# A Flamingo block: the last attention batch in an order of its own, its last pair's sums on VectorE

## The reference

```python
x = x + tanh(g_xattn[0]) * xattn(ctx, layernorm(x), Wq, Wkv, Wout, gm, bm, gl, bl)
x = x + tanh(g_ffn[0]) * ffn(layernorm(x), W_fc, W_proj)

def xattn(x, latents, ...):             # here x is ctx, latents is layernorm(x)
    xn = layernorm(x, gm, bm); ln = layernorm(latents, gl, bl)
    q = ln @ Wq;  k, v = split(concat([xn, ln]) @ Wkv)     # 8 heads of 64
    sim = (q / scale) @ k.T;  attn = softmax(sim - max(sim))
    return (attn @ v) @ Wout
def ffn(x, W_fc, W_proj):
    y = square(relu(x @ W_fc.T)) @ W_proj.T
    # five steps: mem = 0.9*mem + y - reset*1.0, spike = mem > 1.0; the mean of the spikes is returned
```

## Time and profile before

| | us |
|---|---|
| median of 3 runs | 1161.47 (1161.38 to 1162.35) |
| the profiled execution, its own time | 1163.12 |
| its span, first to last instruction | 1161.3 |
| of it: up to the end of the output projection of b = 6, the loop's last | 722.8 |
| the last batch (b = 7), to the start of `up(0, 2)` | 102 |
| the feed-forward part from there | 336.5 |

### The profile page before, as it was taken

The page is one execution under the profiler, slowest core; times in us unless marked ns, Lnnn a source line. Parts: engine busy times, 40 slices in busy tenths (PEclk is TensorE's granted clock), DMA queues, the critical chain, the costliest instruction groups (busy, mean ns, idle before and its releaser), DMA issues.

```text
span 1161.3 us, 19261 instructions
## 1 busy us (share of the span) xinstructions
PE 1082.1 (93%) x7117; PEld 886.2 (76%) x7117; DVE 763.2 (66%) x1138; ACT 535.6 (46%) x999; POOL 376.5 (32%) x336
## 2 busy tenths in 40 slices
PE   2999999999999999999999999865899999999992
PEld 2987887877877877877887887643688788788991
DVE  4247877877777776787687686655433556456498
ACT  4346745844845754754764764332333322322321
POOL 1003433443353353353344434343112122122232
PEclk9789999999999999999999999977899999999996
DMA  5300201200101101101100000121430100200201
GB/s 171 106 23 1 70 1 32 69 0 32 69 0 32 60 9 32 49 19 32 36 33 29 3 0 23 46 82 57 132 109 1 37 1 19 73 1 6 87 2 54
DMA packets 31334, 47.42 MB, mean 41 GB/s; under 512 B 2240, under 2 KB 10448, under 8 KB 31296
## 3 DMA queue, kind: packets, MB, share of 16 engines
q1 hardware_dynamic: 31296, 46.91, 12.5%
HBM read 39.56 MB, written 7.34 MB: 40 GB/s over the span
## 4 chain that ended last, share of the span: by engine, by line
PE 87%; DVE 7%; DMA 2%; POOL 1%; ACT 1%; issue 1%; SPq 0%; DVEq 0%; ACTq 0%; POOLq 0%
PE work L421 50%; PE score L729 11%; PE heads_out L540 8%; PE score L504 8%; PE score L436 2%; PE maxes L661 2%; PE heads_out L549 1%; PE maxes L526 1%; PE maxes L516 1%; DMA xin<-in_ctx 1%; DVE neuron L1385 1%; DVE neuron L1383 1%; POOL dsum L1452 1%; DVE spikes L1381 1%; PE score L421 1%
## 5 line engine op out<-in xcount | busy, mean ns | idle before, releaser
L1452 POOL TENSOR_TENSOR dsum<-dsum,probs 125x448 f32<-125x448 f32 (+1 forms) x192 | 235.9, 1229 | 15.1
L1449 POOL TENSOR_TENSOR dsum<-probs 125x448 f32<-125x448 f32 x32 | 37.0, 1157 | 468.8 <-ACT probs L807 468.8
L421 PE MATMUL work<-wv,xT 128*125 128x512 f32 (+1 forms) x768 | 188.7, 400 | 0.0
L421 PE MATMUL work<-xT,wk 128*128 128x488 f32 (+1 forms) x768 | 188.2, 396 | 0.0
L421 PE MATMUL work<-zT,wf 128*128 128x512 f32 (+1 forms) x768 | 168.5, 371 | 13.2 <-DVE wf L1208 12.2
L421 PEld LDWEIGHTS work<-wv,xT 128*125 128x125 f32 (+1 forms) x768 | 139.0, 184 | 37.4 <-issue 2.3
L421 PEld LDWEIGHTS work<-xT,wk 128*128 128x128 f32 x768 | 142.7, 191 | 31.1 <-issue 4.6
L729 PE MATMUL score<-hT,wp 128*128 128x512 f32 (+1 forms) x768 | 163.8, 363 | 0.6 <-DVE hT L1404 0.6
L421 PEld LDWEIGHTS work<-zT,wf 128*128 128x128 f32 x768 | 134.9, 193 | 37.4 <-issue 14.1
L801 ACT ACTIVATE probs<-score 125x448 f32<-125x448 f32 (+1 forms) x256 | 119.9, 549 | 75.3 <-PE score L504 75.1
L1494 POOL TENSOR_TENSOR h<-relu 128x512 f32<-128x512 f32 (+1 forms) x64 | 71.5, 1118 | 247.0 <-ACT relu L1030 242.6
(11 more groups left out here) (135 smaller groups left out, 1312.8 us busy)
## 6 DMA issues: line engine op xcount, KB each, us to landing
xin<-in_ctx SPq DMA_DIRECT2D x48, 250.0 KB
neuron<-in_L_ffn_W_fc SPq DMA_DIRECT2D x16, 256.0 KB, 4.5
neuron<-in_L_ffn_W_proj SPq DMA_DIRECT2D x16, 256.0 KB, 2.7
xin<-in_x SPq DMA_DIRECT2D x16, 224.0 KB, 9.8
xres<-in_x SPq DMA_DIRECT2D x16, 224.0 KB, 2.6
x_scratch<-xres SPq DMA_DIRECT2D x16, 224.0 KB, 2.3
zt<-x_scratch SPq DMA_DIRECT2D x3, 1024.0 KB, 5.7
fin<-x_scratch SPq DMA_DIRECT2D x3, 1024.0 KB, 5.6
```

What stands on the lines that cost most here:

```text
L421: mm = pe.matmul(bank, lhs(i, k), rhs(j, k), start=(n == 0), stop=(n == len(passes) * chunks - 1))
L1449: pool.tensor_tensor(total[0:CT], tile(0), tile(1), ALU.add).then_inc(dchain, 1)
L1452: pool.tensor_tensor(total[0:ROWS[t]], total[0:ROWS[t]], tile(t), ALU.add).then_inc(dchain if t < TILES - 1 else dsum_done, 1)
```

## The change

Four things are changed, all in or next to the last batch.

1. SP issues `load_z(0, False)` directly behind the loop, ahead of `residual(NA - 2)`, and without the wait for `tr_done`.
2. PE, ACT and DVE have lists of their own for the last batch. DVE makes only the statistics of group 0; ACT makes the negated means, the variance plus epsilon and the four normalisations, and POOL one product more (`nmr`). On PE, `max_transposes(1)` and `max_rows(1)` come ahead of values 4 and 5; `max_transposes(2)`, `max_rows(2)` ahead of the third scores; `max_transposes(3)` and `max_rows(3)` ahead of `up(0, 1)` and of `attend(2)`. On ACT, `heads_hi(1)` moves from ahead of the last pair's first copies to behind the last exponentials, and the copy of value tile 3 to behind `exponentials(1)`. On DVE, `normalise(1)` moves to behind `subtract(7)`.
3. The last pair's exponentials are summed by DVE (`last_sums`, four instructions) instead of POOL's seven.
4. The last pair's value products and totals go to the bank `maxes`, so `attend(3)` no longer waits for `on_done`.

```diff
@@ sync
-            residual(NA - 2, False)
+            load_z(0, False)
+            residual(NA - 2, False)
...
-            sp.wait_ge(tr_done, NA * 2 * DC)
-            load_z(0, False)
@@ tensor, last_batch
-                now_until_queries(b)
+                max_transposes(b, 1)
+                values(b, 4)
+                max_rows(b, 1)
+                values(b, 5)
...
+                max_transposes(b, 2)
                 attend(b, 1)
+                max_rows(b, 2)
                 totals(b, 1)
-                max_transposes(b, 2)
                 scores(b, 3, 0, last=True)
-                max_rows(b, 2)
                 scores(b, 3, 1)
                 up(0, 0, False)
+                max_transposes(b, 3)
+                max_rows(b, 3)
+                up(0, 1, False)
                 attend(b, 2)
                 totals(b, 2)
-                max_transposes(b, 3)
-                up(0, 1, False)
-                max_rows(b, 3)
-                attend(b, 3)
-                totals(b, 3)
+                attend(b, 3, maxes)
+                totals(b, 3, maxes)
@@ scalar, last_batch
+                exponentials(b, 1)
+                copy_values(b, 3, 4, 5)
...
+                heads_hi(b, 0)
+                group_hi(0, 0, 1, 2, 3)
+                split_weights(0)
+                copy_scores(b, 3, 0, 1)
+                exponentials(b, 4)
+                split_weights(1)
+                copy_scores(b, 3, 2, 3)
+                exponentials(b, 5)
+                exponentials(b, 6)
+                exponentials(b, 7)
+                heads_hi(b, 1)
+                split_weights(2, 3)
+                heads_hi(b, 2)
...
@@ vector
+            def last_sums(b):
+                v = probs[:, 2:4, :]
+                dve.wait_ge(exp_done, b * HEADS + HEADS)
+                dve.tensor_tensor(top[0:CT], v[0:CT, :, 0:2 * L], v[0:CT, :, 2 * L:4 * L], ALU.add)...
+                dve.tensor_tensor(top[0:CT], top[0:CT], v[0:CT, :, 4 * L:6 * L], ALU.add)...
+                dve.tensor_tensor(top[0:LT], top[0:LT], v[0:LT, :, 6 * L:8 * L], ALU.add)...
+                dve.tensor_tensor(dsum[0:CT, 2:4, :], top[0:CT, :, 0:L], top[0:CT, :, L:2 * L], ALU.add)...
@@ vector, last_batch
+                group_lo(0, 0, 1, 2, 3)
+                subtract(b, 4)
+                split_weights(0)
+                folds(b, 3, 1)
+                subtract(b, 5)
+                folds(b, 3, 2, 3)
+                maxima(b, 3)
+                split_weights(1)
+                query_maxima(b, 3)
+                subtract(b, 6)
+                subtract(b, 7)
+                normalise(b, 1)
+                heads_lo(b, 1)
+                last_sums(b)
+                split_weights(2)
+                normalise(b, 2)
+                heads_lo(b, 2)
+                split_weights(3)
+                normalise(b, 3, maxes)
+                heads_lo(b, 3)
+                split_weights(4, 5, 6, 7)
```

More of the change, by code:

```diff
@@ L633, in last_batch @@
             def last_batch(b):
-                now_until_queries(b)
+                max_transposes(b, 1)
+                values(b, 4)
+                max_rows(b, 1)
+                values(b, 5)
+                keys_queries(b, 2, (2,))
+                values(b, 6)
+                values(b, 7)
+                attend(b, 0)
+                totals(b, 0)
+                scores(b, 2, 0)
+                keys_queries(b, 3, (0,))
+                scores(b, 2, 1)
+                keys_queries(b, 3, (1, 2))
                 for i in range(4):
@@ L909, in batch @@
                 copy_scores(b, 2, 2, 3)
[L910 to L911 removed]
+                layer_norm(b + 1, 1)
                 kq_hi_parts(b, 3, 1)
[L913 to L927 removed]
                 hi_chunks(b + 1, 0, 0)
@@ L1209, in split_weights, with last_batch, batch @@
                                       ALU.subtract).then_inc(fw_lo, 1)
-            def batch(b, last):
-                if not last:
-                    statistics(b + 1, 0)
-                    statistics(b + 1, 1)
-                else:
-                    group_statistics(0, False)
+            def last_batch(b):
+                query_maxima(b, 1)
+                group_moments(0, False)
+                subtract(b, 2)
+                kq_lo_parts(b, 2, 2)
+                subtract(b, 3)
+                latent_values(b, 6)
+                latent_values(b, 7)
+                normalise(b, 0)
+                folds(b, 2, 1)
+                kq_lo_parts(b, 3, 0)
+                folds(b, 2, 2, 3)
+                maxima(b, 2)
+                kq_lo_parts(b, 3, 1, 2)
+                heads_lo(b, 0)
+                query_maxima(b, 2)
+                group_lo(0, 0, 1, 2, 3)
[19 more added lines that the diff above has]
+                split_weights(4, 5, 6, 7)
+                for i in range(2):
+                    gated_residual(b, i)
+            def batch(b):
+                statistics(b + 1, 0)
+                statistics(b + 1, 1)
                 query_maxima(b, 1)
@@ L1347, in _ @@
             with dve.Fori(0, NA - 1) as b:
[L1348 to L1349 removed]
+                batch(b)
+            last_batch(NA - 1)
             def neuron_op(g, n, last):
@@ L1470, in batch @@
                 else:
-                    inverse_root(g_ve, 1, g_rstd, 0, 4)
-                for p in range(1, PAIRS):
+                    inverse_root(g_ve, 1, g_root, 0, 4)
+                    pool.wait_ge(g_root, 1)
+                    pool.tensor_tensor(nmr[:, 0:4], nmu[:, 0:4], rstd[:, 0:4], ALU.mult).then_inc(g_rstd, 1)
+                for p in range(1, PAIRS - 1 if last else PAIRS):
                     denominators(b, p)
```

117 lines of the change are left out of this document (52 added, 65 removed).

## The result

| us | before | after |
|---|---|---|
| median of 4 runs | 1161.91 (1161.38 to 1165.62) | 1134.9 (1134.71 to 1135.9) |
| profiled execution | 1163.12 | 1135.09 |
| its span | 1161.3 | 1133.3 |

The ratio is 0.9763, with a 95% interval of 0.9741 to 0.9784. The forecast was 1132.7, with a range of 1128 to 1140.

A forecast was written before the change was run, and what follows sets the result against it. TensorE's waits in the last batch's 102 us, a third idle and paid twice through a lower clock, were the bound. +0.75 - 5.05 + 0.5 - 23.3 - 1.7 = -28.8 from 1161.47 gave 1132.7, range 1128 to 1140.

The forecast's parts named there:

- To `attend(0)`: Start of the last batch: value tile 3 later, +0.75; no wait for zt or qmax and faster values 7, -5.05.
- To the last scores: From attend(0) to the last pair's scores: TensorE already full, only max_rows(2) comes in, +0.5 us.
- To the last exponential: From the last scores to the end of the last exponential: 17.7 us in place of 41.0, -23.3, VectorE's chain setting it.
- three moves: Basis of the -23.3: normalise(1) behind the subtractions, heads_hi(1) behind the exponentials, maxima ahead of attend(2).
- To the projection: From the last exponential to the output projection: 13.0 us in place of 14.7, -1.7, the tree's saving mostly lost to queueing.
- The projection: Last batch's output projection: 3.1 us of idle time ahead of it remain, so it keeps 7.20 us, no change.
- A: Rival on TensorE's granted clock: full clock gives 1130.6, inside the main forecast's 0.72; low clock gives 1139, chance 0.09.
- the middle case: Main sum's clock level: attend(2) at half-clock price, 5.17 us, attend(3) at 3.25 and the projection at 7.20, giving 1132.7.
- B: Rival: GpSimd's pair 2 sums run on under VectorE's tree, tree and splits cost +4.5 to +6, 1138; chance 0.09.
- The rule: VectorE instructions with two SBUF inputs contend with active GpSimd; the tree would then cost some 4.5 us more.
- C: Rival: the zt load is not early, statistics still wait, the -5.05 goes, 1137.7; chance 0.03.
- D: Rival: feed-forward part starves on late weight pieces; small loss 1138, chance 0.04; full loss about 1165, chance 0.02.

The follow-up runs named there:

- e1: Kernel before with only the load of group 0's rows moved directly behind the loop, ahead of the residual: median 1158.46 us, ratio 0.9952 to before.
- e3: Changed kernel with the last pair's sums back on GpSimd (seven instructions): median 1135.29 us, ratio 0.9759 to before.
- e9: Changed kernel with an own tile for each of the last two divisions, heads_lo(1) and splits moved behind them: median 1136.2 us, ratio 0.974 to before.
- e5: Changed kernel with normalise(1), heads_lo(1) and heads_hi(1) back at their earlier places, TensorE's list kept: median 1138.08 us, ratio 0.9766 to before.
- e6: As e5, with TensorE's list back too, attend(2) and its totals ahead of the last maxima: median 1150.2 us, ratio 0.9871 to before.
- e7: Changed kernel with the last pair's four sums done twice, 4.0 us more VectorE work: median 1140.2 us, ratio 0.9772 to before.
- e8: Changed kernel with twelve unused products added ahead of attend(2) and twelve behind the last totals: median 1134.62 us, ratio 0.9748 to before.
- e10: Changed kernel with the edits of e8 and e9 together, six products instead of twelve behind the last totals: median 1132.32 us, ratio 0.9717 to before.
- e4: Changed kernel with the last pair's value products and totals back in bank heads_out, tree kept: median 1138.32 us, ratio 0.9771 to before.

## Why the prediction was right

The forecast held in its sum and in its parts, each within 1.2 us.

- *To `attend(0)`*, -4.06 for -4.30. Right in sum. The second half of the projection of b = 6 waits 0.52 for value tile 3 and begins 3.56 behind the first, where the sum had 2.9 + 0.75; a first maximum beside GpSimd's chain added 0.21 in the transposes. The 5.05 I put down to the load and to the early `max_transposes(1)` together; by e1 the load alone gives 5.3, so that move was not needed for it.
- *To the last scores*, +0.56 for +0.5.
- *To the last exponential*, -24.51 for -23.3. Right in its chain, and 1.2 too small, 0.9 of it by one number: the second split was charged 1.61 because GpSimd runs beside it. It took 0.69 at 767.14. GpSimd's first sum, started at 767.00, took 1.82 where the same sum took 1.14 at 737.68: it paid. The Trainium skill, SBUF — State Buffer, "SBUF: two separate sides", has the pair of ports as an exclusive lock, which goes to the one that starts first while the other waits for the whole instruction. The length fits, 0.68 more for a split of 0.69. Who came first the rows leave open: GpSimd's record starts 0.14 ahead of the split's, but VectorE's second maximum, which also has two SBUF inputs, was then still running, until 767.2. The thirteen instructions of VectorE otherwise follow each other as added up. The sum had no term for TensorE here: in e3 and e9 the first up-product at the lower clock held the transposes, and the stretch took 0.6 more.
- The prediction said that this stretch rests on three moves. They give 15.2 of its 24.5: by e5 the division of pair 1, with `heads_hi(1)` and `heads_lo(1)`, 3.8; by e6 the maxima ahead of `attend(2)` 11.4. The other 9.3, from 41.06 in before to 31.72 in e6, come by the traces from a move that the prediction used but did not count: the splits of pieces 0 and 1 stand earlier in VectorE's list. In e6 the first up-product starts 7.1 behind the last scores, in before 16.5, behind a wait of 8.87 for its split, and the 3.35 ahead of the second is gone too. This is read from the two traces; no run undoes that move by itself. The same holds for the moves of the first two maxima and of the normalisation to ScalarE.
- *To the projection*, -2.20 for -1.7. `attend(2)` took 4.93 for the 5.17 charged; its totals took 0.58 in place of 1.01 and ended 5.5 behind the last exponential, not 6.3. The tree ended at 5.3 for 5.0 and the split behind it at 5.9, so it was VectorE's queue that held `normalise(2)`, and not TensorE as in my sum. That the tree's gain is largely given back was right (e3: 1.0 or nothing remains); e7 shows VectorE as the bound, 4.03 of 4.0.
- *The projection*, +1.18 for 0. Wrong, and covered by the other terms: it waits 3.58 and took 8.38 at a granted clock of 0.66, where it had 7.20 at 0.79. I had taken the level from one row; the traces of this study give 5.80 to 8.56. That -28.8 comes so near to -29.04 is in part luck: two misses of 1.2 with opposite signs.
- *The median.* 1132.7 was 2.2 too low. I subtracted a stretch of the profiled execution, 1163.12, from a median of 1161.47. From its own time it would have been 1134.3. The head of the program moves by more than this, so the 2 us are not a finding.

The rivals. A, the clock: the middle case came, a slow `attend(2)` and `attend(3)` at the full clock (3.23), with the projection's 8.38 towards the low side. 1130.6 was not reached. I had put 0.7 of it down to an earlier start of the projection; in e8 `attend(2)` ran at the full clock and the start did not move. B, GpSimd under the tree: it did not happen, by 0.17 us (776.15 against 776.32) where I had 1.3; in e10 it did, and cost 0.83 on one sum. The rule of the Trainium skill, GPSIMD Engine Reference, Specifications, that VectorE's instructions with two SBUF inputs contend with GpSimd, thus agrees with the traces in e10 and e3 (1.92 for 1.09, 1.61 for 0.69), but not every such meeting costs VectorE anything (0.69 at 767.14). C and D fell: the load was issued at 638.58, and the feed-forward part took 336.5 to the tenth.

## What to carry to other kernels

Where engines run fixed lists, add the critical chain up instruction by instruction from one queue's rows, and ask of each instruction in it whether its consumer is urgent: moving two short TensorE steps ahead of work that could wait gave 11 us, a faster algorithm for the sums gave 1 or nothing. The worth of a faster step is read from what its engine's queue does meanwhile: the same tree was worth 4 us in one order and at most 1 in the other. Two near bounds have to be lifted together: own tiles and a busy TensorE gave 0.2 and 1.0 us each and 4.6 us as a pair, part of that by the clock. And compare a stretch that no edit touches before reading a difference of half a microsecond: here one moved by 0.6.

## What was not expected of the hardware

Behind the same wait the granted clock came out differently: the projection took 5.80, 7.20 and 7.85 behind waits of 3.17, 3.18 and 3.18 (e4, before, e3), 7.34 behind 2.37 (e8) and 5.80 behind 1.66 (e10). So the length of the wait alone does not decide. The projection repeats in the two traces of the changed kernel (8.38 and 8.40), yet the same instructions do not always get the same level: the first up-product took 3.02 in both and 4.08 and 4.41 in e3 and e9, which differ from them only further on. What decides was not tried. And when VectorE and GpSimd meet with two SBUF inputs each, the price may fall on either: VectorE 0.69 and GpSimd 1.82 in after, VectorE 1.61 for the split at 776.80 in e3, beside GpSimd's six sums of 1.30 each.
